# A third bank for row scores and two for transposed scores in an attention tower

## The chip, the cores and the metric

The kernel runs on one core of one Trainium2 chip. The metric is the time of one execution on the device, in microseconds (us). The kernel before takes 625.67 us, the median of three runs (624.74 to 625.75).

## What is computed

Four sequences of 512 tokens, 256 wide, go through one layer of a tower: an embedding gather, a local attention with a residual, and then full attention plus a mixture of experts with a residual. The attentions have 16 heads of 16 columns.

```python
h = take(W, x, axis=0)
h = h + local_attention(layernorm(h)) @ Wo + bo      # window 128, one window back, causal
z = layernorm(h)
q, k, v = split(z @ W_qkv + b_qkv)
attn = softmax(q @ k.T / sqrt(16)) @ v               # full: 512 x 512 for each head
gate = softmax(z @ W_gate + b_gate); top 2 of 8 experts
out = h + attn + sum of the two experts' outputs times their gates
```

## The kernel before, in words

The work is a row of eight **stages**, one for each sequence and kind of attention, in the order local 0, local 1, local 2, full 0, local 3, full 1, full 2, full 3 (here numbered 0 to 7; `STAGES`). A stage has 16 **units** (4 groups of 4 heads, times 4 tiles of 128 keys). Each unit is one **slot** of an order written out by hand for every engine; all other work (projections, layer norms, the experts' matmuls, the transposes) is laid into the two half slots of a slot (`PREPS`, `half_slot_jobs`). Semaphores alone tie the engines together; each engine runs its own instructions in order.

The softmax needs the maximum of each row before its exponential. So each head's scores are computed twice:

- **Row scores** (`row_scores`, L1458): queries on partitions. TensorE (PE) writes one bank `SC` for each 128 queries (L1469 in a full stage, L1474 and the mask L1477 in a local one). VectorE (DVE) reduces the bank to the negative maximum (`maxima`: L978 full; L983, L986 local). Four row tiles of a head make a full stage's slot, two a local one's. They run 6 or 7 slots ahead (`LEAD`), so the rows of the next stage begin within the stage before. In the slots u = 10 to 15 of the last stage there are no rows left.
- **Transposed scores** (`scores`, L1481): keys on partitions, with the maximum already folded in as two more rows of the operands. PE writes one bank `ST` (L1491 full, 4 banks a unit; L1497 local, 2 banks a unit). ScalarE (ACT) takes the exponential of the bank into `prob` (`exps`: L843 full, L846 local). PE then multiplies `prob` with V into `OB` (`times_v`, L1518), a unit later in full stages, two units later in local ones.

`SC` is a ring of two banks, `ST` one of three; `OB` and the two banks `R`, through which all other work goes, make eight. Row tile r waits until the maxima of row tile r-2 are done (L1463). Transposed bank n waits until the exponential of bank n-3 is done (L1488).

What PE issues in a full slot (`slot`, L1522), in order: banks e = 0 and e = 1 of `ST`; a row tile; the first half slot's jobs with a row tile among them (after them if they have nothing to be put between); banks e = 2 and e = 3 of `ST`; a row tile; `times_v` of the unit before; the second half slot's jobs with a row tile. In a local slot there is one `ST` bank in each half.

The other lines that the prediction names: L1400 and L1386 are experts' matmuls, L1298 and L1313 projections, L1285 the transposes of the layer norm's output `xn` (DVE, L943), L1408 the transpose of `shift` (the maxima of a group of heads, DVE L995 and L997), L1415 the transpose of `OT` (copied from `OB` by ACT, L829). L789 and L784 are ACT's parts of the projections' splitting, L951 DVE's. L1055, L1057 and L1050 belong to the gate. L1117 and L1092 are DVE steps of the routing.

Of the kernel before, what the change touches and what calls it, by code (L numbers as in the profile page):

```python
# [12 lines left out]
F32 = mybir.dt.float32  # L13
# [7 lines left out]
P = 128  # L21
B = 4
T = 512
# [26 lines left out]
BANKS = (2, 4)  # L50
PV_LAG = (2, 1)
WARM = 6
START_ROWS, START_SHIFT = 27, 31
# [71 lines left out]
def maxima_up_to_row(r):  # L125
    s = next(i for i in range(len(STAGES)) if ROWS_BEFORE[i] <= r < ROWS_BEFORE[i + 1])
    return maxima_up_to(s, r - ROWS_BEFORE[s])
# [135 lines left out]
def tower(nc, x, tok_w, wq, bq, wk, bk, wv, bv, wo, bo, wqkv, bqkv, wg, bg, wexp, bexp, out):  # L263
    with ExitStack() as ctx:
# [29 lines left out]
        QS = [sb(f"QS{k}", [P, H, T], BF16) for k in (0, 1)]  # L294
        KS = [sb(f"KS{k}", [P, H, T], BF16) for k in (0, 1)]
# [9 lines left out]
        neg_max = [sb(f"neg_max{k}", [P, NT, H]) for k in (0, 1)]  # L305
# [50 lines left out]

        SC = [ctx.enter_context(nc.psum_tensor(f"SC{i}", [P, T], F32)) for i in (0, 1)]
        ST = [ctx.enter_context(nc.psum_tensor(f"ST{i}", [P, T], F32)) for i in range(3)]
        OB = ctx.enter_context(nc.psum_tensor("OB", [P, T], F32))
# [31 lines left out]
        s_max = sem("maxima")  # L391
# [6 lines left out]
        s_prob = sem("probabilities")  # L398
# [379 lines left out]
        def _(act):  # L778
# [52 lines left out]
            def exps(s, u, e):  # L831
                kind = STAGES[s][0]
                n = SCORES_BEFORE[s] + BANKS[kind] * u + e
# [6 lines left out]
                act.wait_ge(s_st_ps, n + 1)  # L840
                src = ST[n % 3]
                if kind == FULL:
# [71 lines left out]
        def _(dve):  # L914
# [55 lines left out]
            def maxima(s, k):  # L970
                kind = STAGES[s][0]
                n = TILES[kind]
                head, i = k // n, k % n
                r = ROWS_BEFORE[s] + k
                own_max, bank = neg_max[s % 2], SC[r % 2]
                dve.wait_ge(s_sc_ps, r + 1)
# [264 lines left out]
        def _(pe):  # L1241
# [216 lines left out]
            def row_scores(s, k):  # L1458
# [3 lines left out]
                r = ROWS_BEFORE[s] + k  # L1462
                if r >= 2:  # L1463
                    pe.wait_ge(s_max, maxima_up_to_row(r - 2))
                if head % 8 == 0 and i == 0:
                    pe.wait_ge(s_stacked[s % 2][head // 8], STACK_LOADS * (s // 2 + 1))
                bank, Q, K = SC[r % 2], QS[s % 2], KS[s % 2]
                if kind == FULL:
# [12 lines left out]
            def scores(s, u, e):  # L1481
# [3 lines left out]
                if kt == 0 and e == 0:  # L1485
                    pe.wait_ge(s_shrow, 32 * (G * s + g + 1))
                if n >= 3:
                    pe.wait_ge(s_prob, n - 2)  # L1488
                keys, bank, Q, K = slice(kt * P, (kt + 1) * P), ST[n % 3], QS[s % 2], KS[s % 2]
                if kind == FULL:  # L1490
# [88 lines left out]
```

## Time and profile before

| | |
|---|---|
| time, median of three runs | 625.67 us |
| the profiled execution's own time | 632.04 us |
| its span, first to last instruction | 630.3 us |
| mean granted TensorE clock in it | 0.954 |
| PE busy | 565.0 us, 90% |
| DVE busy | 422.8 us, 67% |
| ACT busy | 296.5 us, 47% |
| GpSimd busy | 182.0 us, 29% |
| stage 0 / 1 / 2 / 3 begin at | 64.5 / 113.7 / 166.7 / 223.1 us |
| stage 4 / 5 / 6 / 7 begin at | 293.7 / 360.3 / 458.5 / 550.1 us |

A row of the trace is one instruction or several of the same line that follow each other: its start, the time they take together, engine, line, what is written and read, how many, and in brackets how long the engine was idle before and what ended that. PE stands for the matmuls and PEld for the weight loads that go ahead of them. A stage begins here where its first transposed bank is written. The granted clock 1.00 is TensorE's 2.4 GHz, 0.50 is 1.2 GHz.

### The profile page before, as it was taken

How to read it: one execution, taken by the hardware profiler on the slowest of the kernel's cores; microseconds unless marked ns; L12 is line 12 of the kernel's file. 1: busy time of each engine (PE TensorE's matmuls, PEld its weight loads, DVE VectorE, ACT ScalarE, POOL GpSimd, SP SyncE). 2: the span in 40 equal slices, each digit the busy share in tenths (PEclk: the TensorE clock that was granted, in tenths of full speed). 3: DMA queues.
4: the chain of work that ended last, by engine and by line, in shares of the span. 5: the costliest groups of instructions: out<-in, count | busy, mean ns of one | idle time of the engine just before them, and what ended most of it. 6: DMA issues, size and time to landing. Idle time of an engine off the chain costs nothing.

```text
span 630.3 us, 9948 instructions
## 1 busy us (share of the span) xinstructions
PE 565.0 (90%) x3445; PEld 303.3 (48%) x3445; DVE 422.8 (67%) x941; ACT 296.5 (47%) x558; POOL 182.0 (29%) x237
## 2 busy tenths in 40 slices
PE   3787899889999998999798899989999989999996
PEld 3343555555565434445453355544535455544452
DVE  6636757575867887667558876856865566677842
ACT  0322446444635564567344353534555445444444
POOL 5463345222422511022223232401132423033201
PEclk9967799899989999999797899999988999999999
DMA  6477437242344226533215216413157788213311
GB/s 173 122 172 165 78 76 193 46 88 67 111 85 80 89 84 152 134 81 106 68 39 165 67 52 158 113 32 88 50 165 181 211 244 223 80 29 123 118 50 35
DMA packets 42945, 69.23 MB, mean 110 GB/s; under 512 B 7176, under 2 KB 36496, under 8 KB 39824
## 3 DMA queue, kind: packets, MB, share of 16 engines
q1 hardware_dynamic: 38656, 56.01, 34.8%
q0 software_dynamic: 4224, 12.59, 6.9%
q8 instruction: 28, 0.46, 0.3%
q14 instruction: 21, 0.17, 0.1%
q10 hardware_dynamic: 16, 0.01, 0.0%
HBM read 45.25 MB, written 23.07 MB: 108 GB/s over the span
## 4 chain that ended last, share of the span: by engine, by line
PE 71%; DVE 16%; issue 5%; ACT 3%; DMA 3%; SPq 1%; POOL 1%; ACTq 0%; DVEq 0%
PE OB L1518 12%; PE R L1400 9%; PE R L1298 9%; PE SC L1469 8%; PE ST L1491 7%; DVE neg_max L978 5%; PE R L1313 5%; PE R L1386 3%; PE SC L1474 3%; PE ST L1497 2%; PE R L1346 2%; PE R L1415 2%; DMA QS<-shiftT 2%; DVE neg_max L986 2%; PE SC L1477 2%
## 5 line engine op out<-in xcount | busy, mean ns | idle before, releaser
L978 DVE TENSOR_REDUCE neg_max<-SC 128x1 f32<-128x512 f32 x256 | 171.1, 687 | 87.9 <-PE SC L1469 84.6
L843 ACT ACTIVATE prob<-ST 128x512 f32<-128x512 f32 x256 | 136.8, 599 | 127.4 <-PE ST L1491 122.5
L1518 PE MATMUL OB<-prob,VS 128*32 128x512 f32 (+2 forms) x1024 | 109.4, 501 | 0.1
L1469 PE MATMUL SC<-KS,QS 96*128 96x512 bf16 x256 | 98.6, 394 | 9.1 <-DVE neg_max L978 6.9
L846 ACT ACTIVATE prob<-ST 128x512 f32<-128x512 f32 (+1 forms) x128 | 68.4, 543 | 77.2 <-PE ST L1497 75.1
L714 POOL TENSOR_SCALAR_AFFINE_SELECT prob<-prob 128x512 f32<-128x512 f32 x64 | 40.9, 640 | 151.6 <-ACT prob L846 151.5
L1491 PE MATMUL ST<-QS,KS 98*128 98x512 bf16 x256 | 79.0, 386 | 2.0 <-ACT prob L843 1.9
L986 DVE TENSOR_REDUCE neg_max<-SC 128x2 f32<-128x512 f32 x64 | 44.1, 689 | 27.2 <-PE SC L1477 26.9
L1474 PE MATMUL SC<-KS,QS 96*128 96x256 bf16 (+1 forms) x256 | 57.9, 279 | 3.3 <-DVE neg_max L983 2.0
L983 DVE TENSOR_REDUCE neg_max<-SC 128x1 f32<-128x128 f32 (+1 forms) x128 | 39.6, 351 | 26.9 <-PE SC L1477 26.6
L1477 PE MATMUL SC<-mask_q,ident_bf 128*128 128x128 bf16 x256 | 53.9, 232 | 0.0
L1497 PE MATMUL ST<-QS,KS 98*128 98x256 bf16 (+1 forms) x256 | 48.5, 272 | 4.7 <-DMA QS<-shiftT 4.7
L1469 PEld LDWEIGHTS SC<-KS,QS 96*128 96x128 bf16 x256 | 25.1, 98 | 52.4 <-DVE neg_max L978 34.3
L700 POOL TENSOR_TENSOR parts<-rest,parts 128x512 bf16<-128x512 f32 x32 | 37.3, 1167 | 39.1 <-ACT parts L789 22.5
L784 ACT ACTIVATE parts<-R,qk_bias 128x512 bf16<-128x512 f32 x32 | 22.0, 686 | 54.8 <-PE R L1298 53.4
L1491 PEld LDWEIGHTS ST<-QS,KS 98*128 98x128 bf16 x256 | 24.8, 99 | 32.3 <-ACT prob L843 11.2
L951 DVE SCALAR_TENSOR_TENSOR rest<-R,qk_bias,parts 128x512 f32<-128x512 f32 x32 | 23.9, 748 | 24.0 <-ACT parts L784 17.3
L1474 PEld LDWEIGHTS SC<-KS,QS 96*128 96x128 bf16 x256 | 26.0, 104 | 28.8 <-DVE neg_max L983 10.6
L724 POOL TENSOR_TENSOR h<-h,AO 128x256 f32<-128x256 f32 x15 | 10.8, 725 | 98.0 <-DVE AO L1020 70.3
L1518 PEld LDWEIGHTS OB<-prob,VS 128*32 128x32 f32 x1024 | 20.5, 110 | 36.9 <-issue 33.2
L1298 PE MATMUL R<-xT_full,w_qkv 128*128 128x512 f32 x64 | 33.0, 608 | 3.0 <-DVE VS L963 3.0
L1140 DVE SCALAR_TENSOR_TENSOR h<-R,comb,h 128x256 f32<-128x256 f32 x64 | 27.8, 475 | 8.8 <-PE R L1400 8.8
(148 smaller groups left out, 804.7 us busy)
## 6 DMA issues: line engine op xcount, KB each, us to landing
scratch<-parts SPq DMA_DIRECT2D x96, 128.0 KB
QS<-scratch SPq DMA_DIRECT2D x16, 384.0 KB, 5.3
KS<-scratch SPq DMA_DIRECT2D x16, 384.0 KB, 4.5
QS<-scratch SPq DMA_DIRECT2D x16, 256.0 KB, 3.6
KS<-scratch SPq DMA_DIRECT2D x16, 256.0 KB, 4.2
x_sorted<-ys SPq DMA_DIRECT2D x24, 128.0 KB, 3.4
xs<-x_sorted SPq DMA_DIRECT2D x12, 256.0 KB
y_sorted<-ys SPq DMA_DIRECT2D x12, 256.0 KB
```

The source lines that it names most:

```text
L843: act.activation(prob[:, u % 2, e, :], src[:, :], ACT.Exp, scale=SCALE).then_inc(s_prob, 1)
L846: act.activation(prob_local[:, u % 2, u // 2 % 2, 2 * e:2 * e + 2, 0:w], src[:, :].rearrange("p (i w) -> p i w", i=2)[:, :, 0:w], ACT.Exp, ...
L978: dve.tensor_reduce(own_max[:, i, head:head + 1], bank[:, :], AX.X, ALU.max, negate=True).then_inc(s_max, 1)
L986: dve.tensor_reduce(own_max[:, 2:4, head], bank[:, :].rearrange("p (w k) -> p w k", w=2), AX.X, ALU.max, negate=True).then_inc(s_max, 1)
L1298: mm = pe.matmul(bank[:, :], w, xT_of(p)[:, c, :], start=(c == 0), stop=(c == NC - 1))
L1400: mm = pe.matmul(bank[:, t % 2 * D:(t % 2 + 1) * D], xT_full[b % 2][:, c, t * P:(t + 1) * P], w_exp[n % W_RING][:, c, :], start=(c == 0), ...
L1469: pe.matmul(bank[:, :], Q[0:SHIFT_ROW, head, i * P:(i + 1) * P], K[0:SHIFT_ROW, head, :], start=True, stop=True).then_inc(s_sc_ps, 1)
L1474: pe.matmul(bank[:, first:last], Q[0:SHIFT_ROW, head, w * P:(w + 1) * P], K[0:SHIFT_ROW, head, max(w - 1, 0) * P:(w + 1) * P], start=(w % ...
L1477: mm = pe.matmul(bank[:, last - P:last], ident_bf[:, :], mask_q[:, :], start=False, stop=(w % 2 == 1), skip_group_check=True)
L1491: mm = pe.matmul(bank[:, :], K[0:KROWS, g * GH + e, keys], Q[0:KROWS, g * GH + e, :], start=True, stop=True)
L1497: mm = pe.matmul(bank[:, i * 2 * P:i * 2 * P + w], K[0:KROWS, head, keys], Q[0:KROWS, head, kt * P:kt * P + w], start=(i == 0), stop=(i == 1),
L1518: mm = pe.matmul(OB[VW * i:VW * (i + 1), columns], VS[s % 3][:, kt, v:v + VW], p_of, start=(kt == 0), stop=(kt == NT - 1), skip_group_chec ...
```

## The change

The two rings get their lengths from two names. `SC` goes from two banks to three, `ST` from three to two, and the waits, the bank chosen and the bank read follow. Nothing else is moved: the eight banks stay eight, and every engine issues the same instructions in the same order. Both rings serve the local stages as well as the full ones.

```diff
+SC_RING, ST_RING = 3, 2
...
-        SC = [... nc.psum_tensor(f"SC{i}", [P, T], F32)) for i in (0, 1)]
-        ST = [... nc.psum_tensor(f"ST{i}", [P, T], F32)) for i in range(3)]
+        SC = [... nc.psum_tensor(f"SC{i}", [P, T], F32)) for i in range(SC_RING)]
+        ST = [... nc.psum_tensor(f"ST{i}", [P, T], F32)) for i in range(ST_RING)]
...  exps (ACT)
-                src = ST[n % 3]
+                src = ST[n % ST_RING]
...  maxima (DVE)
-                own_max, bank = neg_max[s % 2], SC[r % 2]
+                own_max, bank = neg_max[s % 2], SC[r % SC_RING]
...  row_scores (PE)
-                if r >= 2:
-                    pe.wait_ge(s_max, maxima_up_to_row(r - 2))
+                if r >= SC_RING:
+                    pe.wait_ge(s_max, maxima_up_to_row(r - SC_RING))
...
-                bank, Q, K = SC[r % 2], QS[s % 2], KS[s % 2]
+                bank, Q, K = SC[r % SC_RING], QS[s % 2], KS[s % 2]
...  scores (PE)
-                if n >= 3:
-                    pe.wait_ge(s_prob, n - 2)
-                keys, bank, Q, K = slice(kt * P, (kt + 1) * P), ST[n % 3], QS[s % 2], KS[s % 2]
+                if n >= ST_RING:
+                    pe.wait_ge(s_prob, n - ST_RING + 1)
+                keys, bank, Q, K = slice(kt * P, (kt + 1) * P), ST[n % ST_RING], QS[s % 2], KS[s % 2]
```

## Rows read from the trace of the kernel before

**Rows 1.** The page: busy time of the engines, and the chain that ended last.
```profile
PE 565.0 (90%) x3445; PEld 303.3 (48%) x3445; DVE 422.8 (67%) x941; ACT 296.5 (47%) x558; POOL 182.0 (29%) x237
PE 71%; DVE 16%; issue 5%; ACT 3%; DMA 3%; SPq 1%; POOL 1%; ACTq 0%; DVEq 0%
```

**Rows 2.** The page's group of the exponentials: busy, mean ns | idle before, what ended it.
```profile
L843 ACT ACTIVATE prob<-ST 128x512 f32<-128x512 f32 x256 | 136.8, 599 | 127.4 <-PE ST L1491 122.5
```

**Rows 3.** The waits of the whole run: who for whom, us, times, longest.
```profile
PEld SC L1469 <- DVE neg_max L978: 34.3, 63, 1.4
...
PEld ST L1491 <- ACT prob L843: 11.2, 22, 0.8
...
PE SC L1469 <- DVE neg_max L978: 6.9, 14, 1.1
...
PE R L1285 <- DVE xn_local L943: 5.9, 6, 3.4
...
PE SC L1474 <- DVE neg_max L983: 2.0, 2, 1.5
```

**Rows 4.** The waits of 600 to 622 us, stage 7 from slot 10 on.
```profile
PEld ST L1491 <- ACT prob L843: 4.9, 6, 0.8
```

**Rows 5.** The timeline of 606 to 608.5 us, slot 11 of stage 7.
```profile
606.34 2.06 ACT L843 ACTIVATE prob<-ST 128x512 f32<-128x512 f32 x4 [1.63 <-PE ST L1491]
...
606.99 0.39 PE L1491 MATMUL ST<-QS,KS 98*128 98x512 bf16 x1 [0.32 <-ACT prob L843]
```

**Rows 6.** The timeline of 621.4 to 625.9 us, the tail.
```profile
624.13 0.16 PEld L1518 LDWEIGHTS OB<-prob,VS 128*32 128x32 f32 x8 [0.99 <-ACT prob L843]
```

**Rows 7.** The timeline of 555 to 557.6 us, slot 1 of stage 7.
```profile
555.58 2.06 ACT L843 ACTIVATE prob<-ST 128x512 f32<-128x512 f32 x4 [1.81 <-PE ST L1491]
...
555.97 0.65 PE L1491 MATMUL ST<-QS,KS 98*128 98x512 bf16 x2
556.22 0.10 PEld L1491 LDWEIGHTS ST<-QS,KS 98*128 98x128 bf16 x1 [0.38 <-ACT prob L843]
...
556.70 0.39 PE L1469 MATMUL SC<-KS,QS 96*128 96x512 bf16 x1
```

**Rows 8.** The waits of 282 to 293.7 us, slots 13 to 15 of stage 3.
```profile
PEld ST L1491 <- ACT prob L843: 1.0, 3, 0.4
```

**Rows 9.** The timeline of 212 to 223.5 us, the end of stage 2, PE and DVE.
```profile
217.71 0.39 PE L1469 MATMUL SC<-KS,QS 96*128 96x512 bf16 x1 [0.75 <-DVE neg_max L978]
...
221.06 0.39 PE L1469 MATMUL SC<-KS,QS 96*128 96x512 bf16 x1 [0.34 <-DVE neg_max L978]
...
222.28 0.39 PE L1469 MATMUL SC<-KS,QS 96*128 96x512 bf16 x1 [0.26 <-DVE neg_max L978]
```
**Rows 10.** The same stretch, DVE alone.
```profile
216.97 2.47 DVE L978 TENSOR_REDUCE neg_max<-SC 128x1 f32<-128x512 f32 x4
220.31 0.69 DVE L978 TENSOR_REDUCE neg_max<-SC 128x1 f32<-128x512 f32 x1 [0.86 <-PE SC L1469]
```

**Rows 11.** The timeline of 243 to 256.5 us, slots 5 to 7 of stage 3.
```profile
245.46 0.39 PE L1469 MATMUL SC<-KS,QS 96*128 96x512 bf16 x1 [1.10 <-DVE neg_max L978]
...
256.25 0.69 DVE L978 TENSOR_REDUCE neg_max<-SC 128x1 f32<-128x512 f32 x1 [1.09 <-PE SC L1469]
```

**Rows 12.** The timeline of 332.6 to 344 us, stage 4, PE.
```profile
335.33 0.39 PE L1469 MATMUL SC<-KS,QS 96*128 96x512 bf16 x1 [1.11 <-DVE neg_max L978]
...
338.21 0.61 PE L1469 MATMUL SC<-KS,QS 96*128 96x512 bf16 x1 [0.86 <-DVE neg_max L978]
```

**Rows 13.** Busy time by stretches: PE, PEld, DVE, ACT, POOL, then PEclk.
```profile
332.60:336.20 3.60, 1.94 (x17) 0.65 (x15) 3.53 (x7) 1.76 (x5) 3.02 (x4) 1.00 0.67 202
336.20:339.60 3.40, 2.54 (x11) 0.85 (x9) 3.23 (x6) 1.90 (x4) 0.49 (x1) 0.51 0.36 135
339.60:343.10 3.50, 3.35 (x18) 1.59 (x18) 1.74 (x5) 0.66 (x2) 0.63 (x1) 0.50 0.42 128
...
550.10:600.00 49.90, 49.09 (x255) 24.40 (x254) 39.30 (x80) 23.55 (x45) 15.88 (x17) 1.00 0.27 85
```

More of the change, by code:

```diff
@@ L355, in tower @@
         w_rows = sb("w_rows", [P, EXPERT_TILES], I32)
-        SC = [ctx.enter_context(nc.psum_tensor(f"SC{i}", [P, T], F32)) for i in (0, 1)]
-        ST = [ctx.enter_context(nc.psum_tensor(f"ST{i}", [P, T], F32)) for i in range(3)]
+        SC = [ctx.enter_context(nc.psum_tensor(f"SC{i}", [P, T], F32)) for i in range(SC_RING)]
+        ST = [ctx.enter_context(nc.psum_tensor(f"ST{i}", [P, T], F32)) for i in range(ST_RING)]
         OB = ctx.enter_context(nc.psum_tensor("OB", [P, T], F32))
```

## The prediction

> **What bounds the kernel.** I read the page first: PE is busy for 90% of the span and holds 71% of the chain that ended last, DVE 16% [rows 1]. The kernel is a PE stream with many other engines just behind it. A change that makes no instruction shorter can act only through what PE waits for, so I read the waits next. In all, weight loads of full row scores waited 34.3 us for a maximum, in 63 places, and those of transposed scores 11.2 us for an exponential, in 22 [rows 3]. These are not lost times: a weight load runs ahead of its matmul, and PE itself stood idle 6.9 us before L1469 and 2.0 us before L1474 [rows 3]. They say only that the row ring is the tighter one. Then I took the windows in which each kind of wait lies, and their timelines. The row waits lie mostly at the ends of stages 2 and 4 and within stage 3, where DVE carries the rows beside a layer norm or the gate; the exponential's waits lie at the end of stage 3 and, above all, in stage 7, whose half slots hold little else for PE. A wait counts for the end of the kernel unless PE meets another, later one behind it.
>
> **The part that loses: ST from three banks to two.** Bank n now waits for the exponential of n-2 and not n-3. Banks e = 2 and e = 3 follow e = 0 and e = 1 closely where a half slot is thin; e = 3 waited for the exponential of e = 0 and now waits for that of e = 1. Four exponentials take 2.06 us and one of them 0.60 [rows 2, 5], so they start 0.49 us apart ((2.06 - 0.60) / 3), and e = 3 comes 0.49 us later. e = 2 takes the place that e = 3 had, so it costs nothing more.
>
> - Slots 10 to 15 of stage 7 have no rows. PE goes from e = 3 straight into times_v. Six such waits stand there [rows 4]: the first exponential starts at 606.34 and ends at 606.94, e = 3 starts at 606.99 [rows 5]; the second ends at 607.43, so e = 3 starts at 607.48. Nothing else holds PE in these slots. Five of them cost 0.49 us each. In the last slot the final times_v waits for the last exponential anyway, 0.99 us of weight load [rows 6], and that exponential is ACT's, which is late by only some 0.1 us; the PE stream before it grows by 0.49 of which half is covered: 0.25. Sum 2.7 us.
> - Slots 0 to 9 of stage 7 have a row tile behind e = 3, and that tile waited for a maximum. In slot 1, e = 3 goes at 556.22 and the row at 556.70 [rows 7]. After the change e = 3 goes at 556.72 (555.58 + 0.49 + 0.60 + 0.05) and the row 0.22 later, at 556.94, with no wait for DVE: 0.24 later than before. So the third SC bank takes half of the loss back. Ten slots: 2.4 us.
> - Slots 13 to 15 of stage 3 show the same three waits [rows 8], with a local row tile behind that did not wait: three times 0.49, 1.5 us.
> - Elsewhere, singly: slot 0 of stage 3 (0.23), three slots of stage 3 where only e = 3 is late by 0.09, slots 0 and 15 of stage 6 (0.23 each): 1.0 us. In local stages the halves are far enough apart; I found no bank that would be late by the present times. Bound from below 0, from above 0.22 us of exposed load for each of a few: I take 0.
>
> Sum of the losses: 7.6 us. I hold it to be firm, because the exponential's times and the PE order are those of the trace, and the stretches behind have no other wait.
>
> **The part that gains: SC from two banks to three.** Row tile r now waits for the maximum of r-3. Where DVE has no pause, the third bank lets PE run one maximum ahead, 0.60 us (four take 2.47 us, a pause-free pace of 0.60 [rows 10]), but no faster; where DVE pauses because PE is late, that pause closes. So the gain is bounded by DVE's own pauses, and I take it from them.
>
> - Startup and stages 0 to 2: most row waits are followed at once by the transposes of the layer norm, which wait for DVE's xn (5.9 us of PE idle, six times [rows 3]). They are absorbed. Two single ones in stages 1 and 2 and the startup: 0.4 us.
> - End of stage 2: DVE runs without pause up to 219.44, so PE gains 0.60 at the tile at 217.71 and those about it. DVE then pauses for 0.86 before 220.31, which the 0.60 shortens [rows 9, 10]. The tiles at 221.06 and 222.28 waited too, PE idle 0.34 and 0.26 [rows 9], and behind each the load lies bare for some 0.07 more: 0.40 and 0.33. Sum 1.3 us.
> - Stage 3, slots 5 to 7: PE waits 1.10 at 245.46 and several times after. In its timeline DVE then has no pause until one of 1.09 before 256.25 [rows 11]. That pause is what comes back: 1.1 us, and 0.1 in slot 2.
> - Stage 4, 332 to 343 us: PE waits 1.11 and 0.86 us before two tiles [rows 12]. In 332.6 to 336.2 DVE is busy 3.53 of 3.60; in the next two stretches 3.23 of 3.40 and 1.74 of 3.50 [rows 13]: in all 2.0 us of pauses, the upper bound; the lower is 1.1, PE's lead at 339.6. After PE had stood idle for 1.66 of 3.60 us the granted clock fell to 0.5, 1.2 GHz, for some 6.9 us [rows 13]. With less idle before it, it may not fall. I take 1.6, and 0.4 for a like tile at the stage's end: 2.0 us.
> - Stages 5 and 6: three waits with 0.2 us of real delay each, in part absorbed: 0.4 us.
>
> Sum of the gains: 5.3 us, bounded by 1 us if PE meets another wait each time, and by PE's idle time and more (10 us) if nothing absorbs them.
>
> DVE, ACT, POOL and SP issue what they did. SP and POOL wait on the count of transposed banks for their DMA issues, so those move with PE, later in stage 7 by up to 5 us where only the outputs and gathers are left; their cover is several slots.
>
> **The sum.** 7.6 - 5.3 = 2.3 us later in the profiled execution, whose own time is 632.04 us for a span of 630.3. The median of the runs is 625.67, 1% less, and its slots are the same; I carry the difference over unscaled: **627.9 us**. A measurement of this kernel can tell about 0.2% (1.25 us) from no change, so this is slower.
>
> One rule speaks further against the change. Rows: in slots 0 to 9 of stage 7 the granted clock is 1.00 with a wait in each slot, PE busy 49.09 of 49.90 us [rows 13]. The Trainium skill, TensorE: Matmul & The Clock Gate, section "A second HAM failure mode: psum-queue depth-cycling", says that bf16 matmuls of 512 columns that cycle through PSUM banks can leave PE idle so often between groups that its clock swings between half and full; by it stage 7, with longer waits, would lose its full clock. The trace so far does not bear it out there; rival 3 prices it.
>
> **The rivals.**
>
> 1. **Row waits come back whole, faster.** If DVE isn't what holds PE back, all PE idle ahead of row tiles returns: 6.9 and 2.0 us [rows 3], some 1 us of their lesser kinds, and 1 to 1.5 us of loads exposed. With 7.6 lost, this is 2.5 to 3.5 us faster, **623.0 us** or so; if the clock of stage 4 stays up as well, it is what gets it there. It decides from gains over 9 us. For it: 63 against 22 waits [rows 3]. Against it: DVE's pauses, 0.86, 1.09 and 2.0 us, cap the three largest places [rows 10, 11, 13].
> 2. **The rows give nothing, slower by more.** Each PE lead runs into the next wait for DVE (xn, shift, V). Gains 1 us, losses 7.6: **632.3 us**. For it: six xn waits [rows 3]. Against it: DVE's pauses ended by PE's own row tiles.
> 3. **The clock falls once in stage 7.** A stretch like that of stage 4, 6.9 us at 0.5 [rows 13], does what 3.4 us would: 3.4 us more, **631.3 us**. Against it: PE idle per slot rises by 0.5 of 4.5 us only, against 1.66 of 3.60 before the fall in stage 4.
> 4. **Balance.** Gains of 6.4 to 8.8 us meet the losses: **625.7 us**. For it: stage 4 with its clock kept, and small gains that I rounded down. It also covers the change doing nothing of note because waits only change names.
>
> **How the numbers follow.** Forecast (1.3 to 5 us slower) 0.46; rival 1 0.17; rival 2 0.13; rival 3 0.03; rival 4 0.21. Slower by over 0.2%: 0.46 + 0.13 + 0.03 = 0.62; within 0.2%: 0.21; faster: 0.17. The range leaves half of rival 1 and half of rival 2 out: 623.3 to 631.8.
>
> **What would show it.** In the profile after: waits of L1491's loads for L843 rise from 11.2 us to some 20 or more; those of L1469 for L978 fall to a third or less; in slots 10 to 15 of stage 7 a slot is 0.49 us longer, in slots 0 to 9 0.24; stage 7 is 5 us longer in all; stages 2 to 4 together are some 2 us shorter, and DVE's pauses of 0.86 and 1.09 are gone. It is wrong if stage 7 keeps its length (then another wait covered the exponential), or if stages 2 to 4 shrink by more than 5 us (then PE, not DVE, set the pace there).

## The result and the profile after

The changed kernel takes **633.65 us** (median of 4 runs, 633.18 to 636.17) beside 625.71 us of the kernel before on the same chip: ratio 1.0115, 95% interval 1.0084 to 1.0147. Three more series of it gave 1.0104, 1.0103 and 1.0116, so I take 1.011 for it below, 6.9 us. (The two medians of this first series differ by 7.9 us; the ratio rests on all runs.) The forecast was 627.9, with a range of 623.3 to 631.8. The side was right, the size was not: 6.9 us slower, not 2.3.

The page of the changed kernel: busy time, the chain that ended last, the exponentials and the row matmuls (lines are one further down than in the kernel before).

```profile
span 631.4 us, 9948 instructions
PE 562.8 (89%) x3445; PEld 302.2 (48%) x3445; DVE 423.7 (67%) x941; ACT 298.2 (47%) x558; POOL 181.7 (29%) x237
PE 67%; DVE 14%; ACT 7%; DMA 5%; issue 5%; POOL 1%; SPq 1%; ACTq 0%; DVEq 0%; POOLq 0%
L844 ACT ACTIVATE prob<-ST 128x512 f32<-128x512 f32 x256 | 138.9, 596 | 125.9 <-PE ST L1492 119.2
L1470 PE MATMUL SC<-KS,QS 96*128 96x512 bf16 x256 | 96.2, 387 | 5.5 <-DVE neg_max L979 5.3
```

Beside [rows 1, 2]: the exponential takes what it took (596 ns, before 599) and the busy sums are within 2.2 us, but ACT holds 7% of the chain and not 3%. Its waits of the whole run, to hold against [rows 3]:

```profile
PEld ST L1492 <- ACT prob L844: 27.7, 52, 1.0
PEld SC L1470 <- DVE neg_max L979: 21.8, 35, 1.8
PE R L1286 <- DVE xn_local L944: 6.9, 10, 3.4
```

Waits for an exponential went from 11.2 us in 22 places to 27.7 in 52, those for a maximum from 34.3 in 63 to 21.8 in 35. Note the last figure of the row line: the longest single wait is 1.8 us, and before it was 1.4. Fewer waits, but a longer one among them, and more before the layer norm's transposes: 6.9 us of PE idle in ten places, before 5.9 in six.

Stage 7 after slot 10, and one slot of it: the waits of 600 to 622 us, then the timeline of 606 to 608.5 us.

```profile
PEld ST L1492 <- ACT prob L844: 7.1, 10, 1.0
PE ST L1492 <- ACT prob L844: 2.7, 5, 0.5
```
```profile
605.81 1.67 ACT L844 ACTIVATE prob<-ST 128x512 f32<-128x512 f32 x3
605.97 0.88 PE L1492 MATMUL ST<-QS,KS 98*128 98x512 bf16 x2 [0.53 <-ACT prob L844]
606.45 0.10 PEld L1492 LDWEIGHTS ST<-QS,KS 98*128 98x128 bf16 x1 [0.39 <-ACT prob L844]
```

In place of six waits [rows 4] stand ten, and the 0.32 us in which PE stood idle before e = 3 [rows 5] are 0.53 before e = 2 and some more before e = 3, whose weight load waited 0.39. The busy times by stretches, to be read against [rows 13]; the seventh figure is the granted clock:

```profile
332.60:336.20 3.60, 3.49 (x26) 1.55 (x23) 3.01 (x7) 2.37 (x5) 1.74 (x3) 1.00 0.66 137
336.20:339.60 3.40, 1.96 (x19) 0.79 (x18) 3.30 (x7) 2.38 (x6) 2.33 (x3) 1.00 0.77 247
339.60:343.10 3.50, 2.76 (x21) 1.30 (x21) 3.46 (x8) 0.92 (x3) 0.64 (x1) 1.00 0.45 139
550.10:600.00 49.90, 48.12 (x245) 23.45 (x244) 38.07 (x76) 21.84 (x41) 15.87 (x17) 1.00 0.28 85
```

Stage 4 keeps its full clock where it had 0.51 and 0.50, and stage 7 keeps it as well. (In this profile stage 4 begins 2.4 us later than in [rows 13], so the same windows hold slightly earlier work. Compared slot by slot, slots 9 to 12 of stage 4 take 11.7 us and took 14.7.) The clock is lost elsewhere: the same view of the changed kernel, of stage 0, the start of stage 1, the stretch to the end of stage 2, and that end; and last the end of the kernel before.

```profile
64.00:112.00 48.00, 43.81 (x378) 25.93 (x375) 31.89 (x82) 25.36 (x49) 22.53 (x30) 0.95 0.47 111
112.00:118.00 6.00, 5.23 (x42) 3.95 (x42) 2.31 (x8) 3.56 (x6) 0.77 (x2) 0.72 0.00 0
118.00:214.00 96.00, 89.60 (x701) 54.23 (x699) 67.22 (x175) 45.95 (x90) 26.32 (x37) 0.96 0.35 83
214.00:222.00 8.00, 6.24 (x47) 2.83 (x47) 6.96 (x11) 4.64 (x9) 6.77 (x9) 0.82 0.36 110
```
```profile
214.00:222.00 8.00, 6.20 (x53) 2.58 (x50) 7.03 (x14) 4.70 (x9) 6.36 (x9) 1.00 0.27 87
```

The 0.72 at the start of stage 1 is no loss by the change: the first profile of the kernel before has it too, and 0.98 from 118 to 214. What the changed kernel has and that profile lacks is a second stretch in the middle of stage 2, at 192 us, and one at its end, at 219.

The two other places of the gain: stage 3, 243 to 259 us, and stage 4, 332 to 344 us, PE's rows that waited.

```profile
250.02 0.39 PE L1470 MATMUL SC<-KS,QS 96*128 96x512 bf16 x1 [0.55 <-DVE neg_max L979]
254.15 0.39 PE L1470 MATMUL SC<-KS,QS 96*128 96x512 bf16 x1 [0.89 <-DVE neg_max L979]
...
337.66 0.39 PE L1470 MATMUL SC<-KS,QS 96*128 96x512 bf16 x1 [0.98 <-DVE neg_max L979]
340.22 0.39 PE L1470 MATMUL SC<-KS,QS 96*128 96x512 bf16 x1 [1.08 <-DVE neg_max L979]
```

DVE's pause of 1.09 us [rows 11] is gone: from 246 to 262 us the timeline lists none for DVE. And in stage 4 PE still waits 0.98 and 1.08 us [rows 12], but the clock doesn't fall.

The length of a stage, taken in the timeline from its first transposed score matmul to that of the next (for stage 7, to the start of the last instruction), gives this table (us, profiled executions; one number where all agree). The third profile of the first column and the fourth of the last are of kernels with another tail in stage 7, told of below, and its row leaves them out:

| stages | kernel before (3 profiles) | 2 banks and 2 (2) | changed (5 profiles) |
|---|---|---|---|
| 0 to 2 | 158.6, 157.0, 157.7 | 158.1, 155.2 | 161.5, 158.1, 158.2, 158.3, 162.6 |
| 3 | 70.6 | 72.6 | 71.2 |
| 4 | 66.6 | 64.8, 66.6 | 63.1, 62.8, 63.1, 63.0, 63.9 |
| 5 and 6 | 189.8, 188.2, 189.2 | 187.8, 187.7 | 187.1, 187.8, 187.9, 186.8, 185.3 |
| 7 | 80.13 | 85.13 | 85.13 |

Stages 3 and 7 repeat to 0.02 us, the others vary, and they vary by the granted clock: a microsecond at 1.2 GHz instead of 2.4 loses up to half of itself, less where PE waits in it anyway. In stages 0 to 2 the length less half of the time at half clock lies between 150.2 and 153.4 us in all twenty profiles, of whatever kernel, though the lengths run from 154.6 to 165.5.

### The profile page after: what moved, and what is told of

Its sections match the earlier page's. It is cut to its first block, busy times and chain, and to the rows that moved or that the text cites. A ratio compares the mean times of both kernels' runs of the same rounds, so it can differ in the third digit from the quotient of the medians.

```text
span 631.4 us, 9948 instructions
## 1 busy us (share of the span) xinstructions
PE 562.8 (89%) x3445; PEld 302.2 (48%) x3445; DVE 423.7 (67%) x941; ACT 298.2 (47%) x558; POOL 181.7 (29%) x237
## 4 chain that ended last, share of the span: by engine, by line
PE 67%; DVE 14%; ACT 7%; DMA 5%; issue 5%; POOL 1%; SPq 1%; ACTq 0%; DVEq 0%; POOLq 0%
PE OB L1519 13%; PE R L1401 9%; PE R L1299 8%; PE SC L1470 7%; PE ST L1492 7%; PE R L1314 5%; ACT prob L844 4%; PE R L1387 3%; PE SC L1475 3%; PE ST L1498 3%; DVE neg_max L979 2%; PE R L1416 2%; DMA QS<-shiftT 2%; PE R L1347 2%; DVE neg_max L987 2%
## 5 line engine op out<-in xcount | busy, mean ns | idle before, releaser
L844 ACT ACTIVATE prob<-ST 128x512 f32<-128x512 f32 x256 | 138.9, 596 | 125.9 <-PE ST L1492 119.2
L1470 PE MATMUL SC<-KS,QS 96*128 96x512 bf16 x256 | 96.2, 387 | 5.5 <-DVE neg_max L979 5.3
L1492 PE MATMUL ST<-QS,KS 98*128 98x512 bf16 x256 | 81.3, 382 | 7.7 <-ACT prob L844 3.9
L715 POOL TENSOR_SCALAR_AFFINE_SELECT prob<-prob 128x512 f32<-128x512 f32 x64 | 40.7, 637 | 152.7 <-ACT prob L847 152.5
L701 POOL TENSOR_TENSOR parts<-rest,parts 128x512 bf16<-128x512 f32 x32 | 37.3, 1168 | 37.4 <-ACT parts L790 21.2
L1492 PEld LDWEIGHTS ST<-QS,KS 98*128 98x128 bf16 x256 | 24.7, 98 | 45.8 <-ACT prob L844 27.7
L1470 PEld LDWEIGHTS SC<-KS,QS 96*128 96x128 bf16 x256 | 24.8, 97 | 38.9 <-DVE neg_max L979 21.8
L725 POOL TENSOR_TENSOR h<-h,AO 128x256 f32<-128x256 f32 x15 | 10.9, 725 | 101.8 <-DVE AO L1021 70.6
```

The lines of the kernel that those rows point to most:

```text
L844: act.activation(prob[:, u % 2, e, :], src[:, :], ACT.Exp, scale=SCALE).then_inc(s_prob, 1)
L1470: pe.matmul(bank[:, :], Q[0:SHIFT_ROW, head, i * P:(i + 1) * P], K[0:SHIFT_ROW, head, :], start=True, stop=True).then_inc(s_sc_ps, 1)
L1492: mm = pe.matmul(bank[:, :], K[0:KROWS, g * GH + e, keys], Q[0:KROWS, g * GH + e, :], start=True, stop=True)
```

## The experiments

Ratios are to the kernel before on the same chip, with their 95% interval; "clock" is the granted clock averaged over all runs of a series.

**Both kernels again.**

> The kernel before, unchanged, with a profile of its own. The profile that the prediction was read from lasted 632.04 us where the median is 625.7. If that profile was an odd one, this one spans about 624 to 626 us, with a mean granted clock above 0.954, and lacks one or both of the stretches at 0.50 of stages 4 and 5 (336 to 343 and 357 to 363 us). If being profiled costs 6 us of itself, it spans 630 again. Time: the ratio to the kernel before is 1.000 within 0.3%.

> The changed kernel again, with a second profile. Theory 1 (the two rings' lengths act by their waits alone): stage 7 is 85.1 us long again, 5.0 more than before, and stage 2 is not longer than before in this profile; its 2.5 us more were chance. Theory 2 (the third SC bank lets TensorE run ahead of DVE, its idle time gathers in one place and the clock falls): the clock is at 0.50 once more at about 192 us and at about 221 us of stage 2, as in the first profile, and stage 2 is 2 to 3 us longer than before. Time 633 to 634 us under both.

Measured: 628.03 us, 1.002 (0.9996 to 1.0045), and 632.10 us, 1.0104 (1.0061 to 1.0148). The clock over the runs is 0.962 and 0.960. The kernel before had a profiled execution of 632.04 us, 1% over its median; its second one spans 626.6 us with the same slots in stages 3 and 7. It was expected to lack the stretches at half clock of stages 4 and 5; they are there again, at 334 and 355 us, and those at 114 and 469 are not. Of the two stretches that theory 2 put into stage 2 of the changed kernel, the second profile has the one at the end (217 us) and not the one at 192, and the stage is 56.0 us long beside 58.9 in the first profile and 56.4 before. So a single profile of this kernel is a sample of its clock.

**Each half of the change alone.** Two banks for each, the sixth left unused, so that only ST differs from the kernel before and only SC from the changed one.

```diff
-SC_RING, ST_RING = 3, 2
+SC_RING, ST_RING = 2, 2
```

> SC 2 banks, ST 2 banks: the loss alone, without the third SC bank. Theory 1: the third SC bank gave back the 5.3 us of the prediction, so this kernel is 4 to 5 us slower than the changed one, 638 us. Theory 2: the third SC bank gives nothing in sum, since what it gives in waits it takes in the clock: 633 to 634 us, the same as the changed kernel. In both, slots 10 to 15 of stage 7 are each 0.49 us longer than before, and slots 0 to 9 too are 0.24 longer, as the row tile behind the bank no longer waits.

> SC 2, ST 2 a second time, for a firmer number: 634 to 635 us, 7 to 8 us slower than before, and 1 to 2 us slower than the changed kernel. The stretch at 0.50 at 335 us is there and none at 217.

Measured: 634.15 us, 1.0128 (1.0085 to 1.017), and 634.64 us, 1.0127 (1.0084 to 1.017). Taking a bank from the transposed scores costs 8.0 us (forecast 7.6). Giving one to the rows is worth 1.013 - 1.011, about 1.1 us, where I had forecast 5.3; the intervals are wide enough for nothing at all or for twice that. So the third bank did not give back what theory 1 said (638 us). The slots tell more: slots 0 to 9 of stage 7 take 51.25 us before, 53.61 here and 53.60 in the changed kernel. The 0.24 us a slot come from ST alone; I had thought that ST cost 0.49 there and that the third row bank gave half of it back.

**The loss by itself.** Slots 10 to 15 of stage 7 have no rows, so from there all five banks, ST's and SC's, serve the transposed scores in turn (`st_bank`).

```diff
-                src = ST[n % ST_RING]
+                src = st_bank(n)
...
+                if n >= TAIL + ALL:
+                    pe.wait_ge(s_prob, n - ALL + 1)
+                elif n >= TAIL + ST_RING:
+                    pe.wait_ge(s_max, maxima_up_to_row(ROWS_BEFORE[-1] - 1))
```

> The changed kernel, but from slot 10 of stage 7 on, where no row tile is left, the three SC banks join the ST ring (5 banks). It takes away the waits of transposed banks for exponentials there. Where they are lost time, each of five slots loses its 0.49 us of the change and the 0.48 us that were there before, the last slot less: 5 to 6 us faster than the changed kernel, about 628 us, in slots 10 to 15 of stage 7 alone. If another wait stands behind (the experts' weights, DVE's sums into h), it is less than 3 us.

> The kernel before (2 SC, 3 ST), but from slot 10 of stage 7 on the two SC banks join the ST ring. The kernel before also had a wait of 0.48 us in each of those six slots, for the first exponential. Without it: 2.4 to 2.9 us faster than before, all of it in slots 10 to 15 of stage 7 (stage 7 77.3 us long, from 80.1). If the clock or DVE takes it back, less than 1 us.

Measured: on the changed kernel 628.16 us, 1.0022 (0.9993 to 1.0052), so 5.5 us less; on the kernel before 624.54 us, 0.9945 (0.9916 to 0.9974). In the profiles a slot takes 3.78 us where it took 4.28 before and 4.76 changed; stage 7 is 80.0 and 77.7 us. The waits of the changed kernel's tail, over 595 to 618 us here, are down to one:

```profile
PEld ST L1507 <- ACT prob L855: 0.8, 1, 0.8
```

The same edit is worth 2.45 us in stage 7 of the kernel before and 5.1 in that of the changed one. In slots 10 to 15 the wait for the exponential is the loss, and it adds up slot by slot as worked out; for slots 0 to 9 the evidence is the kernel with two banks and two.

**Where the gain went.** A lead of three means that row tile r waits for the maxima of r-3, a lead of two that it waits for those of r-2. First a kernel in which rows have the lead of three only from stage 4 on, then one with it from stage 3 on, and one that lacks it only at the end of stage 2 (the 24 rows of stage 3 issued there).

```diff
-                if r >= SC_RING:
-                    pe.wait_ge(s_max, maxima_up_to_row(r - SC_RING))
+                lead = SC_RING if s > 3 else 2
+                if r >= lead:
+                    pe.wait_ge(s_max, maxima_up_to_row(r - lead))
```

(`s >= 3` in the second; `lead = 2 if s == 3 and k < TILES[FULL] * LEAD[FULL] else SC_RING` in the third. The banks rotate by three in all of them.)

> The changed kernel's banks (3 SC, 2 ST), but the row tiles of stages 0 to 3 wait for the maximum of r-2, as before; only those of stages 4 to 7 use the third bank's lead. Clock theory (TensorE's lead over DVE at the end of stage 2 gathers its idle time in one place, 1.5 us ahead of one row tile, and the clock falls behind it at 217 to 220 us): no stretch at 0.50 near 217 us, stage 2 as long as before or with two SC banks, 56.4 us, stage 3 72.5 us (its 1.3 us of gain gone), stage 4 still 63 us. In sum 0 to 2 us slower or faster than the changed kernel. Waits-only theory: the lead was a pure gain everywhere, and the kernel is 1.7 to 3 us slower than the changed one.

> The changed kernel a third time, beside the others on one chip. If the clock falls at the end of stage 2 by the mechanism named, it is there in this profile too (217 to 220 us at 0.50), stage 7 is 85.1 us and stage 3 71.2 us. Time 5 to 7 us above before.

> 3 SC and 2 ST banks; the row tiles of stages 0 to 2 (local) wait for the maximum of r-2, those of stages 3 to 7 for r-3. If the early lead costs by the end of stage 2 alone, the clock still falls at 217 us and the kernel is within 1 us of the changed one (633). If it costs in the local stages too, by the waits gathered ahead of the layer norm's transposes, it lies between the changed kernel and the one whose lead begins at stage 4 (630.8).

> 3 SC and 2 ST banks; only the 24 row tiles of stage 3 that are issued within stage 2 wait for r-2, all others for r-3. Clock theory for the end of stage 2: no stretch at 0.50 near 217 us, stage 2 not over 56.4 us, stage 3 keeps its 71.2 us, and the kernel is 1.3 us faster than the one whose lead begins at stage 4, so 629 to 630 us, some 3 us faster than the changed one. If the fall there is no cause, it is as slow as the changed kernel, 633.

> The changed kernel with the lead of two rows in stages 0 to 2 and of three from stage 3 on, once more. If the 3.5 us over the changed kernel were real, ratio 1.003 to 1.007 to the kernel before, 629 to 631, mean granted clock over the runs 0.964 to 0.968, and at most 12.5 us of stages 0 to 2 at half clock in the profile. If they were a stroke of luck of one series: 1.009 to 1.012 like the changed kernel, and clock 0.957 to 0.961.

Measured: 630.79 us, 1.0075 (1.0043 to 1.0106), clock 0.967; the changed kernel 633.48, 1.0103 (1.0068 to 1.0138), clock 0.958; from stage 3 on 629.62, 1.0046 (1.0016 to 1.0076), clock 0.965, and again 630.09, 1.0058 (1.0029 to 1.0087), clock 0.964; without it only at the end of stage 2 633.86, 1.0112 (1.0069 to 1.0154), clock 0.959. So the lead makes the kernel slower where it is given to the rows of stages 0 to 2: taking it away there saves (1.011 - 1.0052) 3.6 us, the mean of two series (4.0 and 3.3). I had expected the second kernel between 630.8 and the changed one; it is below both. My first idea, that the end of stage 2 was the culprit, fell with the third kernel: 629 to 630 was expected of it, and it is no faster than the changed one.

From stage 3 on, the third bank gives in sum what was forecast. The mean of the two is 1.0052 beside 1.0128 for two banks and two: 4.7 us. I had 1.2 for stage 3, 2.0 for stage 4, 0.4 for stages 5 and 6 and a part of the 1.3 at the end of stage 2.

**Which stage.** The changed kernel, but with `lead = 2 if s == 0 else SC_RING`, and the same with 1 and with 2; and the changed kernel beside them.

> The changed kernel, but the row matmuls of stage 0 wait for the maximum of row r-2 again; the other seven stages keep r-3. Open is where the 3.5 us lie that the changed kernel (633.1) has over the one without the lead in stages 0 to 2 (629.6). Theory P, one place: one of the three local stages carries nearly all of it, so one of the three runs stands at 629.5 to 630.5 and the other two at 632.5 to 633.5. Theory A, each stage carries its share: each of the three runs takes off about 1.2 us, 631.5 to 632.3. Theory C, the lead only shifts PE's pauses against the stretches in which the clock is granted, so that no single stage owns the loss: the three runs needn't add up to 3.5, and single ones may stand above 633.1, as the run without the lead at the end of stage 2 did. For this one P at stage 0 says 630; its PE pauses in stage 0 (rows wait at slot 6) come back, some 0.5 us of the waits for the DVE maxima.

> The changed kernel, but the row matmuls of stage 1 (the first of them are issued at the end of stage 0) wait for the maximum of row r-2; all others keep r-3. Theory P at stage 1: 630, with PE's clock whole at the start of stage 1, where all five profiles with the lead have a stretch at half clock and four of nine without. Theory A: 631.5 to 632.3. Theory C: anything from 630 to 634.5, and the sum of the three savings is not 3.5.

> The changed kernel, but the row matmuls of stage 2 (the first of them are issued at the end of stage 1) wait for the maximum of row r-2; all others keep r-3, those of stage 3 at the end of stage 2 among them. Theory P at stage 2: 630, and no stretch at half clock near 216 us of the profile, where all five profiles with the lead have one and none of nine without. Theory A: 631.5 to 632.3. Theory C: anything from 630 to 634.5, and the stretch near 216 may stay, since what DVE and POOL do at the end of stage 2 (the shift at L996 and L998 beside POOL's mask and difference, one pause of PE of 1.48 us) is the same.

> The changed kernel once more, on the chip of the three runs beside it: 633.1 by all theories (632.0 to 634.2), ratio 1.009 to 1.013, mean granted clock over its runs 0.957 to 0.960, and in the profile at least 12 us of stages 0 to 2 at half clock with a stretch near 216.

Measured: 632.97 us, 1.0114 (1.0059 to 1.0168); 632.04, 1.0087 (1.0051 to 1.0123); 633.01, 1.0101 (1.0056 to 1.0146); the changed kernel 633.58, 1.0116 (1.0076 to 1.0156). Theory P fell, at least for 3.5 us in one place. The savings by ratio, 0.1, 1.8 and 0.9 us, with intervals wider than they are, leave A open as a sum of 2.8 and don't exclude C. Against a fixed place speaks that the stretches at half clock move: near 216 us the first two have one and the third none, near 113 us the third has one of 6.8 us and the first two none.

Cut into slots, the profiles show one more place, the middle of stages 1 and 2. With a lead of three in the stage's rows, PE comes through slot 6 earlier and meets DVE's layer norm in slot 7. Stage 2, slot 7: first the changed kernel (second run), then the one with the lead from stage 3 on (second run), by engine.

```profile
187.71 1.27 POOL L715 TENSOR_SCALAR_AFFINE_SELECT prob<-prob 128x512 f32<-128x512 f32 x2
187.77 1.35 DVE L944 TENSOR_SCALAR xn_local<-h,mean,rstd 128x256 f32<-128x256 f32 x2 [0.28 <-POOL rstd L697]
188.63 0.30 PE L1286 MATMUL R<-ident,xn_local 128*128 128x128 f32 x1 [0.44 <-DVE xn_local L944]
189.18 0.33 PE L1286 MATMUL R<-ident,xn_local 128*128 128x128 f32 x1 [0.25 <-DVE xn_local L944]
```
```profile
187.93 0.63 POOL L715 TENSOR_SCALAR_AFFINE_SELECT prob<-prob 128x512 f32<-128x512 f32 x1
188.00 1.04 DVE L944 TENSOR_SCALAR xn_local<-h,mean,rstd 128x256 f32<-128x256 f32 x2 [0.28 <-POOL rstd L697]
```

POOL's two masks now follow each other, DVE's two operations beside them take 1.35 us and not 1.04, and PE waits for `xn` three times, 1.27 us in all, where it waited once, 0.59. At full clock slots 6 and 7 take 0.3 us longer in either stage (6.79 for 6.48 us in stage 1, 6.62 for 6.30 in stage 2): here the lead is a loss even without the clock. And in 9 of the 18 cases (a stage 1 or 2 of some profile) with a lead of three a stretch at half clock begins in slot 7 or 8, in none of the 22 with a lead of two. The profiles of these three runs fit: the first has such a stretch in stage 1, the second in stage 2, the third in stage 1. How much of the 3.6 us stands there, the medians don't tell.

What does not move at the end of stage 2 is the pause. Both timelines: first two banks and two (second run), then the changed kernel; PE's wait for the row, what DVE did, and POOL beside it.

```profile
211.53 0.17 DVE L996 CAST shift<-neg_max 128x16 bf16<-128x16 f32 x1
211.67 0.63 POOL L715 TENSOR_SCALAR_AFFINE_SELECT prob<-prob 128x512 f32<-128x512 f32 x1 [0.76 <-ACT prob L847]
211.74 0.59 DVE L998 TENSOR_TENSOR shift<-neg_max,shift 128x16 bf16<-128x16 f32 x1
212.25 2.47 DVE L979 TENSOR_REDUCE neg_max<-SC 128x1 f32<-128x512 f32 x4
212.99 0.39 PE L1470 MATMUL SC<-KS,QS 96*128 96x512 bf16 x1 [0.75 <-DVE neg_max L979]
```
```profile
216.99 0.64 POOL L715 TENSOR_SCALAR_AFFINE_SELECT prob<-prob 128x512 f32<-128x512 f32 x1 [0.28 <-ACT prob L847]
217.32 0.33 DVE L996 CAST shift<-neg_max 128x16 bf16<-128x16 f32 x1
217.59 1.15 POOL L701 TENSOR_TENSOR parts<-rest,parts 128x512 bf16<-128x512 f32 x1
217.68 1.09 DVE L998 TENSOR_TENSOR shift<-neg_max,shift 128x16 bf16<-128x16 f32 x1
218.69 2.47 DVE L979 TENSOR_REDUCE neg_max<-SC 128x1 f32<-128x512 f32 x4
219.43 0.61 PE L1470 MATMUL SC<-KS,QS 96*128 96x512 bf16 x1 [1.48 <-DVE neg_max L979]
```

With three row banks PE comes early, and POOL's mask starts after 0.28 us of idle and not 0.76; DVE's two short operations meet POOL's two long ones. Each ends when POOL's does: L996 at 217.65 (L715 at 217.63), L998 at 218.77 (L701 at 218.74). They take 1.42 us and not 0.76. And PE, a row further ahead, waits out all of it in one piece: 1.48 us after one of 0.28, in place of 0.71 and 0.75. All ten profiles with a lead of three there and nothing filled in have this pause to the hundredth, and eight of them a stretch at half clock that begins between 215 and 220 us; all nine with a lead of two have the shorter pauses, and one of them (the kernel without the lead only at the end of stage 2) such a stretch, at 222.

Two of the ten have the pause and no half clock behind it, and they show what the lead is worth there by the waits alone: slots 13 to 15 of stage 2 take 8.90 us in both, and 9.41 with a lead of two. In the other eight they take 10.0 to 11.9. DVE's pause of 0.86 us [rows 10] shows the same: first in the kernel with the lead from stage 3 on (first run), at full clock, then in the changed kernel.

```profile
218.64 0.69 DVE L979 TENSOR_REDUCE neg_max<-SC 128x1 f32<-128x512 f32 x1 [0.27 <-PE SC L1471]
```
```profile
222.82 0.69 DVE L979 TENSOR_REDUCE neg_max<-SC 128x1 f32<-128x512 f32 x1 [1.65 <-PE SC L1470]
```

**The pauses filled.** If the clock's answer to PE's pauses is the loss, then matmuls that compute nothing must bring it back. They write banks that are free and are overwritten next, so the output is unchanged.

```diff
+                if n >= ST_RING:
+                    pe.wait_ge(s_prob, n - ST_RING + 1)
+                if s == 1 and u == 0 and e == 0:
+                    keep_warm(3, ST[n % ST_RING])
                 if kt == 0 and e == 0:
                     pe.wait_ge(s_shrow, 32 * (G * s + g + 1))
-                if n >= ST_RING:
-                    pe.wait_ge(s_prob, n - ST_RING + 1)
...
+                if s == 2 and u == 14:
+                    pe.wait_ge(s_OT, G * s + 3)
+                    keep_warm(2)
                 for step in quarters[2]:
                     row_scores(*step)
```

(`keep_warm(n)` issues n matmuls of 128x256 into a bank. The wait for a free bank moves ahead of the wait for the shift; PE waits for both as before.)

> The changed kernel with five matmuls added whose results are overwritten: three (128x256, f32) into the free ST bank ahead of the first transposed scores of stage 1, where PE waits 1.9 to 2.7 us for the shift's DMA, and two into OB ahead of the row matmul in slot 14 of stage 2, where PE waits 1.48 us for a maximum. Theory clock: it is these pauses that the granted clock answers to, and each stretch at half clock (3.4 us) costs 1.7 us. Then the profile has no stretch at half clock from 112 to 118 us (five of six profiles of the full lead have one) and none from 214 to 222 (six of six have one), the waits themselves are as long or shorter by the filled part, stages 0 to 2 take 155 to 158 us, not 158 to 162.6, and the median is 629.7 (628.7 to 631.0). Theory C (the stretches only move to the next pause): the half-clock time of stages 0 to 2 stays near 17 us and the median at 632.5 to 633.5. Rival, the pauses and not the clock are the loss: no gain, 633.1, since the pauses end when they did.

Measured: 629.40 us, 1.0036 (1.0006 to 1.0067), clock 0.965 and not 0.958: 4.6 us faster than the changed kernel (1.0110 less 1.0036; some 2 to 7 by the intervals), by five matmuls whose results nobody reads. The timeline of PE at the two places, and the stretches:

```profile
110.39 1.56 PE L1280 MATMUL ST<-w_q,ident 128*128 128x256 f32 x6
113.03 0.39 PE L1500 MATMUL ST<-QS,KS 98*128 98x256 bf16 x2 [1.08 <-DMA QS<-shiftT]
...
218.06 1.03 PE L1280 MATMUL OB<-w_q,ident 128*128 128x256 f32 x4
219.71 0.39 PE L1470 MATMUL SC<-KS,QS 96*128 96x512 bf16 x1 [0.62 <-DVE neg_max L979]
```
```profile
64.00:112.00 48.00, 45.63 (x385) 27.29 (x383) 31.56 (x82) 25.39 (x49) 22.69 (x30) 0.94 0.48 111
112.00:118.00 6.00, 4.97 (x58) 3.76 (x60) 3.45 (x11) 4.11 (x9) 1.27 (x2) 1.00 0.01 3
118.00:214.00 96.00, 89.58 (x689) 54.19 (x681) 66.09 (x173) 44.91 (x89) 25.88 (x36) 0.95 0.36 83
214.00:222.00 8.00, 7.10 (x61) 3.60 (x58) 7.25 (x12) 5.10 (x10) 6.50 (x9) 1.00 0.36 113
```

Both places keep 1.00 where the changed kernel had 0.72 and 0.82. The waits end no sooner (the pause of the row is 0.62 behind 1.03 us of filling), so it isn't the pause but what the clock does behind it that was paid for: slots 0 and 1 of stage 1 take 3.48 us where the changed kernel's profiles have 5.0 to 5.1, and slots 13 to 15 of stage 2 take 8.99 where they have 10.0 to 11.4. The rival that the pauses themselves are the loss fell. But in this profile theory C holds as well: stages 0 to 2 take 160.5 us, not the 155 to 158 expected, with 16 us at half clock, as the changed kernel has in the mean, since new stretches stand in slots 7 and 8 of stages 1 and 2 (134 and 192 us); the span is no shorter, 631.5 us. The gain rests on its series of runs, not on this profile. And the kernel before also has a stretch at half clock at the start of stage 1 in one of two profiles; it was not run with the pauses filled. So the run shows what the clock behind two pauses costs, not that it is the lead's loss.

**Versions that beat both.** The five banks given out by a plan: the middle one belongs to the rows only where they wait, to ST else, and in the tail all serve ST.

```diff
+def RING(what, s, u):
+    rows_have_it = s == 4 and u >= 8 or s == 3 and 2 <= u < 9
+    if what == "row":
+        return (0, 1, 2) if rows_have_it else (0, 1)
+    if s == len(STAGES) - 1 and u >= 10:
+        return (3, 4, 2, 0, 1)
+    return (3, 4) if rows_have_it else (2, 3, 4)
```

(The first of the two has only the condition on stage 4.)

> Five banks, the middle one changing hands: it serves the row tiles in slots 8 to 15 of stage 4 only (3 SC, 2 ST there), the transposed scores everywhere else (2 SC, 3 ST), and from slot 10 of stage 7 on all five serve the transposed scores. It takes the one large gain of the change (stage 4, 1.8 to 3.5 us, the stretch at 0.50 at 335 us gone) and none of its losses, and the gain of the tail (2.4 to 2.9). Stage 4 63 to 64 us, stage 7 77.3 us: 4 to 6 us faster than before, about 621 us. If the clock falls elsewhere in exchange, only the 2.4 to 2.9 of the tail remain.

> As the kernel with the bank that changes hands, but the row tiles have it in slots 2 to 8 of stage 3 too. Stage 3 falls from 70.6 to 69.3 to 69.6 us (the 1.2 us of slots 5 to 7, less 0.2 of single waits), the rest stays: 1 us faster than that kernel, 620.5 to 621.5 us, 5 to 6 us faster than before.

Measured: 622.13 us, 0.9916 (0.9886 to 0.9946), and 619.87 us, 0.9886 (0.9847 to 0.9925): 1.1% faster than the kernel before. Both gains and neither loss: stage 3 is 69.4 us and stage 7 is 77.7, and the rows of stages 0 to 2 keep their lead of two. Stage 4 and stage 7 of the second, in stretches:

```profile
332.60:344.00 11.40, 10.93 (x85) 5.14 (x86) 11.06 (x23) 4.76 (x10) 2.55 (x4) 1.00 0.57 154
550.10:600.00 49.90, 49.34 (x263) 25.42 (x263) 37.56 (x78) 24.55 (x48) 14.01 (x15) 1.00 0.32 96
```

## Why the prediction was wrong

- **Stage 7, 5.1 us lost.** Right to a tenth: 85.13 less 80.13 is 5.00; slots 10 to 14 grow by 0.49 each and the last by 0.20. The reason given for slots 0 to 9 was wrong, as told above: the third row bank gives nothing back there.
- **Stage 3, slots 13 to 15, 1.5 us lost, and slots 5 to 7, 1.1 gained.** Right: 0.49 in each of the three; 0.79, 0.18 and 0.23 in the others. DVE's pause was the bound, as worked out from [rows 11].
- **The sum of the losses, 7.6 us.** 8.0 measured by itself.
- **Stage 4, 2.0 us gained.** Undersized, if anything: 63.2 us in place of 66.6 in the means of the table. Nearly all of it is the clock. The stretch at half clock near 335 us is there in all five profiles in which rows have two banks in stage 4, and in none of the fifteen with three, but that one of these has 3.4 us at 339. Less half of its time at half clock, stage 4 takes 57.8 to 58.2 us in all but two profiles (55.6 and 55.8). I had taken the kept clock for a possible part of the gain; it was the gain. PE still waits 0.98 and 1.08 us there.
- **Stages 5 and 6, 0.4 us gained.** 2.1 us in the table's means, 187.0 for 189.1, within what the clock moves them.
- **Startup, stages 0 to 2 and their end, 0.4 and 1.3 us gained. This is the step that failed.** The prediction said "PE gains 0.60 at the tile at 217.71 and those about it" and priced the end of stage 2 at 1.3 us, the stages before it at 0.4, with their other waits "absorbed". The runs show 3.6 us lost by the lead of stages 0 to 2 in place of a gain. At the end of stage 2 the waits alone give 0.5 us (8.90 for 9.41): slot 13 gains the 0.60, slot 15 gains 0.57, but slot 14 loses 0.65, since there PE's two pauses become one twice as long, with DVE's short operations behind POOL. I had not looked at POOL there. In slots 6 and 7 of stages 1 and 2 the lead costs 0.3 us each, for the same kind of reason. By the slots at full clock, stages 0 to 2 with their end are shorter by only 0.1 us in sum. The second and larger part is that the sum had no term for a clock that falls. The five profiles of the full lead have 16 us at half clock in stages 0 to 2 in the mean, the ten with a lead of two in these stages 10; of the difference 3.7 us stand at the end of stage 2 and 1.4 in slots 7 and 8. In length that is 159.7 us for 157.3: 2.4 lost in place of 1.7 gained.
- **Profile to median.** I carried the difference over "unscaled" (625.67 and 2.3 make 628.0; 627.9 is a slip of rounding). The means of the stage table differ by 2.2 us (2.0 + 0.7 - 3.4 - 2.1 + 5.0, stages 0 to 2 first), the runs by 6.9. The rest is the clock again, between the profiled executions and the others: the four profiles of the changed kernel average 0.962, its runs 0.958; the two of the kernel before 0.960, its runs 0.962. (0.004 + 0.002) of 630 us is 3.8, an upper bound: within a series, 0.001 of clock goes with 0.39 us, which makes 2.3. So 1 to 2.5 us stay without a place.
- **The signs.** Stage 7 and the waits for an exponential (27.7 us) came as said. The waits of the row loads did not fall to a third (34.3 to 21.8), stages 2 to 4 of the first profile are 0.3 us shorter and not 2, and of DVE's two pauses that of 1.09 us is gone while that of 0.86 grew to 1.65.

Of the rivals, the second (the rows give nothing, 632.3) has the nearest number, but not by its mechanism: stages 3 and 4 gave all that was forecast, and stages 0 to 2 took it back. The third priced a fall of the clock, 3.4 us, and put it in stage 7 at 0.03. That 3.6 us were lost elsewhere is close to its price by chance: it is several stretches in some executions, not one in all. The rule of the Trainium skill quoted with it (TensorE: Matmul & The Clock Gate, "A second HAM failure mode: psum-queue depth-cycling") isn't borne out where I applied it: stage 7 waits in each slot at 1.00. The falls that came with the change stand behind one pause of 1.48 us (eight of ten profiles) and three waits of 1.27 to 1.36 in sum (nine of eighteen cases). The length of a pause alone doesn't tell: one of 1.44 us, for V at 139 to 145 us, has no fall behind it in any of the twenty profiles.

Open is how the 3.6 us divide among these places. That the clock is the means is supported, not proven: the series with the lead in all of stages 0 to 2 average a clock of 0.956 to 0.960, the three without it there 0.964 to 0.967; for the two with the lead from stage 3 on, at 0.39 us for 0.001, this makes 2.5 of the 3.6 us. That the end of stage 2 has a longer pause with the lead is shown as well, and that the half clock follows is usual and not certain: eight of ten. But the kernel with the lead from stage 3 on has the same pause, in one of two profiles the same stretch, and is still 3.6 us faster, and the three kernels without the lead in one stage each don't add up to it. At the start of stage 1 PE waits for the shift's DMA, 1.85 to 2.4 us in the changed kernel's profiles and 1.25 to 2.4 in those of a lead of two, by when that DMA lands; too few to say that the lead makes it longer.

## What to carry to other kernels

A bank taken from a ring is priced well from the timeline: the times at which the consumer finishes, followed slot by slot, gave the 5 us of stage 7 to the tenth. A bank given to a ring is worth only what the consumer's pauses allow, and here it also made the producer's remaining waits fewer and longer, and moved short operations of other engines onto each other. Before counting such a gain, look where the remaining waits will stand and what the other engines do there, and put a possible fall of the clock into the range at up to half of its stretch; one profile can't tell whether it will come. Where rings need depth at different times, give the spare bank out by stage rather than for good: that was the fastest version here.

## What was not expected of the hardware

- At the end of stage 2 of the changed kernel, two DVE operations of 128x16 took 0.33 and 1.09 us where each takes 0.17 in stage 7 of the same profile (below), ending within 0.03 us of POOL's instruction. A reduction from PSUM beside POOL's L701 (at 211.9 us) took its usual 0.68 us. The Trainium skill, SBUF — State Buffer, section "Who interferes with whom", says that a cast, where it runs in a two-port mode, and a tensor-tensor operation with both inputs in SBUF contend with GpSimd for a shared pair of ports, which locks one of the two out, and that a reduction does not; by that, the trace agrees. In which mode L996 ran, no run shows.

```profile
557.12 0.17 DVE L996 CAST shift<-neg_max 128x16 bf16<-128x16 f32 x1
...
557.33 0.17 DVE L998 TENSOR_TENSOR shift<-neg_max,shift 128x16 bf16<-128x16 f32 x1
```

- 2.6 us of matmuls whose results nobody reads made the changed kernel 4.6 us faster by the ratios; the granted clock stayed at 1.00 over the two pauses that they fill.
- Runs of one and the same kernel spread by some 0.3% (standard deviation), and with the granted clock: within a series the time is 0.39 us longer for each 0.001 less of it, over all 262 runs taken together. A single profile can't carry a difference of 3 us in this kernel; the slots of stages 3 and 7, which repeat to 0.02 us (all but the first slot of stage 3 in one profile, at half clock), can.
